# Attention groups 8 to 47 with P divided before the split, and P times V in four column tiles

## The reference

```
query = q @ w_q.T;  key = k @ w_k.T;  value = v @ w_v.T      # q is layernorm(x), k = v = ctx
scores = einsum("bghnd,bgsd->bghns", query, key) / 32 ** 0.5
scores = where(mask, scores, finfo.min)
attention = softmax(scores, axis=-1)
out = einsum("bghns,bgsd->bghnd", attention, value)
x = x + out.reshape(b, n, 1024) @ w_out.T
x12 = layernorm(x) @ w12.T + b12;  x1, x2 = split(x12, 2)
x = x + (silu(x1) * x2) @ w3.T + b3
```

## Time and profile before

| | |
|---|---|
| three runs | 1041.37, 1043.22, 1044.38 us; median 1043.22 |
| profiled execution, span from first to last instruction | 1040.4 us |
| PE busy | 1017.7 us, 98% of the span |
| DVE, POOL, ACT busy | 661.6, 498.6, 447.3 us (64%, 48%, 43%) |
| chain of work that ended last | PE 87%, DVE 6%, DMA 1%, ACT 1% |
| granted TensorE clock | 9 or more tenths in every slice, mean 0.998 |

### The profile page before, as it was taken

How to read it: one execution, slowest core, us unless ns; L and a number is a source line. 1 busy time by engine, 2 the same in 40 slices (tenths; PEclk the granted TensorE clock), 3 DMA queues, 4 the chain that set the end, 5 groups by cost and what they waited for, 6 DMA issues and landing times.

```text
span 1040.4 us, 21876 instructions
## 1 busy us (share of the span) xinstructions
PE 1017.7 (98%) x8400; PEld 695.6 (67%) x8400; DVE 661.6 (64%) x2080; ACT 447.3 (43%) x983; POOL 498.6 (48%) x476
## 2 busy tenths in 40 slices
PE   7897999999999999999999999999999999999998
PEld 6786868869687696886655544444444888468853
DVE  6789977767787777888646234636864447625431
ACT  6768556557465574664766210123431112202100
POOL 2869923727337273379958596158742301212000
PEclk9999999999999999999999999999999999999999
DMA  9669686998989999789946715494758631974201
GB/s 367 227 160 197 168 216 168 222 247 222 248 211 229 230 245 244 179 236 232 268 94 123 253 71 203 94 345 160 272 200 185 235 112 40 236 230 122 83 31 51
DMA packets 230776, 199.12 MB, mean 191 GB/s; under 512 B 177040, under 2 KB 187280, under 8 KB 225808
## 3 DMA queue, kind: packets, MB, share of 16 engines
q1 hardware_dynamic: 230672, 197.72, 69.0%
HBM read 119.04 MB, written 35.65 MB: 149 GB/s over the span
## 4 chain that ended last, share of the span: by engine, by line
PE 87%; DVE 6%; DMA 1%; ACT 1%; issue 0%; SPq 0%; DVEq 0%
PE bank_dense L1349 52%; PE bank_spare L1349 13%; PE bank_score L1494 6%; PE bank_spare L1494 6%; PE bank_av L1494 3%; PE bank_score L1406 2%; DVE arena_attn L1820 2%; DVE arena_attn L1830 1%; PE bank_av L1424 1%; PE bank_av L1428 1%; PE bank_av L1426 1%; PE bank_dense L1366 1%; DMA k_scratch<-arena_in 1%; PE bank_spare L1358 0%; PE bank_dense L1358 0%
## 5 line engine op out<-in xcount | busy, mean ns | idle before, releaser
L1153 ACT ACTIVATE arena_attn<-arena_attn,arena_in 128x128 f32<-128x128 f32 x512 | 162.7, 391 | 94.6 <-DVE arena_in L1820 93.6
L1349 PE MATMUL bank_dense<-arena_rows,arena_in 128*128 128x256 f16 (+1 forms) x1272 | 175.2, 295 | 1.9 <-POOL arena_in L874 1.0
L936 POOL TENSOR_TENSOR arena_attn<-arena_attn 128x512 f16<-128x512 f32 x89 | 102.6, 1170 | 148.8 <-ACT arena_attn L1160 148.8
L1349 PE MATMUL bank_dense<-arena_attn,arena_rows 128*128 128x512 f16 x768 | 166.4, 379 | 0.0
L1349 PEld LDWEIGHTS bank_dense<-arena_rows,arena_in 128*128 128x128 f16 x1272 | 123.0, 98 | 43.1 <-DVE arena_in L1668 1.6
L1820 DVE CUSTOM_DVE_ANT_0 arena_attn<-bank_score,arena_in 128x128 f32<-128x128 f32 x512 | 143.5, 346 | 0.4 <-PE bank_score L1406 0.4
L1349 PEld LDWEIGHTS bank_dense<-arena_attn,arena_rows 128*128 128x128 f16 x768 | 75.2, 98 | 90.2
L1349 PE MATMUL bank_dense<-arena_out,arena_attn 128*128 128x512 f16 x576 | 127.8, 379 | 0.0
L1349 PEld LDWEIGHTS bank_dense<-arena_out,arena_attn 128*128 128x128 f16 x576 | 55.5, 98 | 63.3
L1349 PE MATMUL bank_spare<-arena_rows,arena_in 128*128 128x256 f16 (+1 forms) x648 | 87.6, 292 | 0.0
L1349 PE MATMUL bank_dense<-arena_out,arena_in 128*128 128x512 f16 x384 | 83.0, 379 | 0.0
(11 more groups left out here) (219 smaller groups left out, 1890.8 us busy)
## 6 DMA issues: line engine op xcount, KB each, us to landing
arena_rows<-x SPq DMA_DIRECT2D x32, 512.0 KB, 6.1
arena_in<-w_scratch SPq DMA_DIRECT2D x64, 256.0 KB, 3.1
arena_attn<-q_scratch SPq DMA_DIRECT2D x48, 256.0 KB, 4.5
arena_rows<-w_t SPq DMA_DIRECT2D x12, 1024.0 KB, 6.2
arena_rows<-ctx_t SPq DMA_DIRECT2D x8, 1024.0 KB, 6.1
q_scratch<-arena_attn SPq DMA_DIRECT2D x16, 512.0 KB, 5.1
x_scratch<-arena_rows SPq DMA_DIRECT2D x16, 512.0 KB, 3.8
arena_out<-x_scratch SPq DMA_DIRECT2D x16, 512.0 KB, 5.9
```

The source lines that it names most:

```text
L936: ins = pool.tensor_tensor(p_split[:, g % 2, u, 1], e[:, g % 2, u], p_split[:, g % 2, u, 0], ALU.subtract)
L1153: ins = act.activation(head, head, ACT.Exp, bias=neg_max[:, g % 2, h:h + 1], scale=-1.0)
L1349: ins = pe.matmul(dst, lhs(a, c), rhs(b, c), start=(c == chunks[0] and n == 0), stop=(c == chunks[-1] and n == 2))
```

## The change

For groups 8 to 47 (`NORMED`, blocks 2 to 6) P is divided by its row sums before it is split. The row sum comes from the accumulator of the exponentials on ACT. In steps 0 and 1 of a block DVE divides (`by_vector`), in steps 2 to 7 POOL (`by_pool`; the reciprocal is a power of -1); P is scaled by 2 to the 14th. `prob_hi` then waits for the division instead of the exponentials. P times V has V as the stationary operand (128 by 32) and P streams (128 columns); the four heads of a group go to four column tiles of the array, and so to four quarters of the partitions, which is the layout that `out_proj` needs. So `weigh(g)` writes a dense bank, takes the place of `turn_attn(g)` in the middle of step `g + 3`, and `divide` and `turn_attn` are gone for these groups. SP's wait for `weigh(g - 2)` in `turn_prob` becomes a wait for this later place.

```diff
+NORMED = range(8, 48)
+P_SCALE = 2.0 ** 14
+def by_vector(g):
+    return g in NORMED and g % GROUPS < 2
+def by_pool(g):
+    return g in NORMED and g % GROUPS >= 2
...
+        def weighed(g):
+            return (s_dense, done("a", g)) if g in NORMED else (s_av, divided_count(g))
...
 def turn_prob(g):
                 if g >= 2:
-                    sp.wait_ge(s_av, g - 1)
+                    sp.wait_ge(*weighed(g - 2))
...
             # POOL
+            def norm_prob(g):
+                n = normed_count(g - 1, by_pool)
+                for u in range(U):
+                    pool.wait_ge(s_exp, 2 * g + u + 1)
+                    pool.tensor_scalar(inv_pool[:, u], p_sum[:, g % 2, u], 1 / P_SCALE, None, ALU.mult).then_inc(s_pinv, 1)
+                    pool.wait_ge(s_pinv, 2 * (U * n + u) + 1)
+                    pool.tensor_tensor(inv_pool[:, u], inv_pool[:, u], minus_one.broadcast_to([P, HPG]), ALU.pow)\
+                        .then_inc(s_pinv, 1)
+                    pool.wait_ge(s_pinv, 2 * (U * n + u) + 2)
+                    heads = e[:, g % 2, u].rearrange("p (j n) -> p j n", j=HPG)
+                    ins = pool.tensor_tensor(heads, heads, inv_pool[:, u].rearrange("p (j o) -> p j o", o=1)
+                                             .broadcast_to([P, HPG, SEQ]), ALU.mult)
+                ins.then_inc(s_pnorm, 1)
                     if GROUPS * (t - 1) + s > PLO_ALONE:
                         prob_lo(GROUPS * (t - 1) + s - 1)
+                    if by_pool(GROUPS * (t - 1) + s):
+                        norm_prob(GROUPS * (t - 1) + s)
...
             # ACT
                     head = e[:, g % 2, u, SEQ * j:SEQ * j + SEQ]
+                    if g in NORMED:
+                        ins = act.activation(head, head, ACT.Exp, bias=neg_max[:, g % 2, h:h + 1], scale=-1.0,
+                                             accum_out=p_sum[:, g % 2, u, j:j + 1])
...
             def prob_hi(g):
-                act.wait_ge(s_exp, 2 * g + 2)
+                if by_pool(g):
+                    act.wait_ge(s_pnorm, normed_count(g, by_pool))
+                elif by_vector(g):
+                    act.wait_ge(s_vnorm, normed_count(g, by_vector))
+                else:
+                    act.wait_ge(s_exp, 2 * g + 2)
...
             # PE, weigh(g)
+                if g in NORMED:
+                    dst = begin("a", g)
+                    terms_of_out = ((v_high, 0), (v_low, 0), (v_high, 1))
+                    for u in range(U):
+                        for n, (v, piece) in enumerate(terms_of_out):
+                            for j in range(HPG):
+                                ins = pe.matmul(dst[DH * j:DH * j + DH, SEQ * u:SEQ * u + SEQ],
+                                                v[:, a % 2, u, m, 0:DH], prob_t[:, g % 2, u, piece, j],
+                                                start=n == 0, stop=n == 2, tile_position=(0, DH * j))
+                    ins.then_inc(s_dense, 1)
+                    return
...
-                    if g >= 3:
+                    if g >= 3 and g - 3 in NORMED:
+                        weigh(g - 3)
+                    elif g >= 3:
                         turn_attn(g - 3)
...
-                    if g >= 2:
+                    if g >= 2 and g - 2 not in NORMED:
                         weigh(g - 2)
...
             # DVE
+            def norm_prob(g):
+                n = normed_count(g - 1, by_vector)
+                for u in range(U):
+                    dve.wait_ge(s_exp, 2 * g + u + 1)
+                    dve.reciprocal(inv_vector[:, u], p_sum[:, g % 2, u]).then_inc(s_vinv, 1)
+                    dve.wait_ge(s_vinv, U * n + u + 1)
+                    heads = e[:, g % 2, u].rearrange("p (j n) -> p j n", j=HPG)
+                    ins = dve.scalar_tensor_tensor(out=heads, in0=heads, scalar=P_SCALE,
+                                                   in1=inv_vector[:, u].rearrange("p (j o) -> p j o", o=1)
+                                                   .broadcast_to([P, HPG, SEQ]), op0=ALU.mult, op1=ALU.mult)
+                ins.then_inc(s_vnorm, 1)
             def divide(g):
+                if g in NORMED:
+                    return
...
                         attn_lo(g - 3)
+                    if by_vector(g):
+                        norm_prob(g)
```

More of the change, by code:

```diff
@@ L302, in later_unit, with normed_count, divided_count @@
     return UNITS * (f - PLAIN) + i
+def by_vector(g):
+    return g in NORMED and g % GROUPS < 2
+def by_pool(g):
+    return g in NORMED and g % GROUPS >= 2
+def normed_count(g, kind=lambda n: n in NORMED):
+    return sum(kind(n) for n in range(g + 1))
+def divided_count(g):
+    return g + 1 - normed_count(g)
 def plo_count(g):
@@ L1362, in turn_attn @@
             def turn_attn(g):
-                pe.wait_ge(s_avread, g + 1)
+                pe.wait_ge(s_avread, divided_count(g))
                 dst = begin("a", g)
```

35 lines of the change are left out of this document (25 added, 10 removed).

## The result

The changed kernel takes 1075.4 us (median of four runs, 1072.0 to 1077.2) against 1043.7 us: the ratio is 1.030, 95% interval 1.026 to 1.033. It is slower by 31.7 us, where 13 were forecast. The profiled execution has a span of 1074.6 us, 34.2 more than that of before.

What follows compares the result with a forecast made beforehand. PE was taken to bound blocks 2 to 6, busy in all of block 3's 64.65 us. The terms -2 + 6 + 1 + 8 = +13 us on 1043.2 gave 1056 us, slower by 1.2%, range 1030 to 1088.

Steps and rivals of the forecast that it cites:

- rival C: Blocks 2 to 6: POOL becomes the bound, its power paying for each column; +47 us, about 1090; chance 0.11.
- A: The forecast itself, the sum of the terms: 1056 us, slower by 1.2%; chance 0.40.
- D: New `weigh` on PE: tiles go one after another, 1.52 us each, +27 us and the stalls, 1085 us; chance 0.13.
- PE's list, -2 us: PE, 40 groups: new `weigh` 0.80 us replaces 0.84 of `weigh` and `turn_attn`; -2 us, between -20 and +27.
- Rival B: New `weigh` on PE: tiles stream side by side, 0.33 us or 0.53 with shape change; faster, 1037 us; chance 0.25.
- Block 2, +6 us: Block 2, steps 0 and 1: DVE's `norm_prob` ahead of the old divisions, 3.0 us a step; +6 us (3.8 to 7.5).
- The +1 us for later blocks: Steps 0 and 1 of the four later blocks: PE waits for DVE only at step 3's output projection; +1 us.
- Step 7, +8 us: Step 7 of five blocks: PE waits 1.6 us for `v_lo`, as ACT is late behind POOL; +8 us (6 to 12).
- `prob_hi` 2.0 us late: End of step 6 on ACT: `prob_hi` starts at 235.2 instead of 233.23, after POOL's division of 2.3 us.
- Hidden work: POOL's list grows from 30.7 to some 58 of 64.65 us a block; no wait of PE while POOL keeps up.
- The load whose lateness I thought covered by DVE's idle time: SP's load behind `turn_prob`: some 2 us late, DVE standing still that long, covered by its 16 us idle a block.
- The sign that I named for C: What would show rival C: POOL's power over 1.5 us and POOL busy over 90% of a block.

Runs made afterwards that it cites:

- clock kept: The changed kernel with PE turning the identity 24 and 12 times in step 7 of blocks 3 to 6: 1071.4 us, ratio 1.028.
- the best version found: Against the change: reciprocals early on DVE, loads and the b12 reduction reordered, only groups 11 to 39 without each block's step 6 changed: 1038.2 us, 0.996.

## Why the prediction was wrong in size

The direction was right, but 13 us were forecast and 31.7 measured, and the mechanism that set the time was rival C's, POOL as the bound, not A's. The time lay in the range because the range had been drawn up to C and D, so this speaks neither for the sum nor for A. By steps, blocks 2 to 6 took 33 us more: the five steps 7 32.3, steps 0 to 3 of block 2 4.0, waits in steps 4 and 5 of blocks 3 to 6 5.3, and the other 31 steps 8.3 less.

1. **PE's list, -2 us.** Wrong value between the right bounds: -10.8 by the run with the tiles alone. I had taken 0.80 us for `weigh` from the pace of the old load and matmul pairs; it takes 0.84 - 0.26 = 0.58, its 24 matmuls being six rounds of four, one round each 57 ns: 14 ns a matmul, below the old pairs' 25. The 0.2 us that I added for the change of the array's shape were near: 0.58 less six rounds of 57 ns leaves 0.24. Rival B's mechanism was right and decided nothing, since PE no longer bound the blocks. The Trainium skill's page "TensorEngine Tiling (Array Packing)", section Instruction Overhead, puts some 60 cycles on each matmul, 25 ns at 2.4 GHz by an estimate from that page. The trace does not agree for tiles side by side: 57 ns for a round of four are 14 ns a matmul, and the measurement decides. The estimate from the Trainium skill's page "TensorE: Matmul & The Clock Gate", Part 3, was 67 ns a round and 0.40 us; the rows above show 57 ns a round, 0.34 us for six.

2. **Block 2, +6 us.** Right in mechanism and near in size (rows below, answer to the earlier trace rows): steps 0 to 3 cost 4.0 us more (6.67 to 7.24, 6.66 to 8.42, 7.34 to 8.64, 9.11 to 9.45). DVE's products took 0.78 and 1.32 us in the first step, 2.4 us with the reciprocals, and not the 3.0 that I took. The +1 us for later blocks was not there.

```profile
120.80 0.78 DVE L1915 SCALAR_TENSOR_TENSOR arena_attn<-arena_attn 128x512 f32<-128x512 f32 x1
...
121.71 1.32 DVE L1915 SCALAR_TENSOR_TENSOR arena_attn<-arena_attn 128x512 f32<-128x512 f32 x1
...
125.01 0.44 PE L1428 MATMUL bank_dense<-arena_in 128*128 128x128 f32 x2 [1.68 <-DVE arena_in L1927]
```

3. **Step 7, +8 us.** This is the step that failed: the five steps 7 took 32 us more. The wait for `v_lo` was as forecast (1.61 us), but ahead of it stood 3.1 us for `scale_rows`, which I had followed in ACT's list and not to PE, and behind it the low clock. The error under both is "`prob_hi` 2.0 us late". It was 5.9 us late, because I let POOL divide the first sequence as soon as its exponentials were there. In POOL's list the division stands behind `prob_lo` of the group before, which waits for that group's `prob_hi`, which waits for its division. The lateness is there at the end of step 2 (7.8 us) and is handed on from step to step; that step 2 alone makes it is not shown, since the run with step 2's division on DVE did not decide.

4. **Hidden work.** "No wait of PE as long as POOL keeps up" was the right condition, and I answered it with POOL's busy time, 58 of 64.65 us (measured: 59.9). What counts is the chain. POOL's groups in block 3 of the change, by line:

```profile
L972 POOL TENSOR_TENSOR arena_attn<-arena_attn 128x512 f16<-128x512 f32 x16 | 18.2, 1157 | 6.1 <-ACT arena_attn L1222 6.1
L985 POOL TENSOR_TENSOR arena_attn<-arena_attn 128x512 f32<-128x512 f32 x12 | 12.5, 1039 | 0.9
L981 POOL TENSOR_TENSOR arena_attn<-arena_attn 128x4 f32<-128x4 f32 x12 | 12.4, 1036 | 1.0
```

POOL waits 6.1 us for `prob_hi` (and 1.4 for `exps`), which in turn wait for POOL; with these answers and the gaps between its operations its list fills the block. The load whose lateness I thought covered by DVE's idle time was not covered either: DVE stood 3.1 us for it in step 4 of its list, and PE up to 1.1 us for `mask_scores` of step 5 behind it.

```profile
226.82 2.29 DVE L1731 TENSOR_REDUCE arena_in<-arena_rows 128x1 f32<-128x2048 f32 x1 [3.10 <-DMA arena_rows<-w_t]
```

5. **Rival C.** Its condition did not come true (the power took 1.04 us, not the 1.63 of a price for each column), and yet POOL became the bound: the formula was nearly right and its threshold was worked out wrongly. 30.7 + 6 x (2n + 1.1) reaches 64.65 us at n = 2.28 us a sequence, that is at a power of about 0.94 us by the same terms (0.19 + 1.05 + 0.1 beside it), not 1.3. My own 1.0 us was past it. The whole division of a sequence took 2.5, and the formula with this gives 30.7 + 6 x 6.1 = 67.3; with the splits drawn out and the gaps it was 70.4 (clock kept) to 71.5. The sign that I named for C, POOL busy in over 90%, was wrong too: 84% was enough.

## What to carry to other kernels

Before work is moved to an engine with much idle time, follow its list once around: if what it is given waits, over another engine, for what it has itself just done, the period of that loop counts, not the busy share, and 84% busy can be full. When a loop is opened by another order, look for the next one, over the buffers (here the two of `e`). And a saving on the engine that bounds the kernel is only paid out as long as it stays the bound: here the tiles were worth 10.8 us alone, nothing beside the division, and 4.7 us in the best version found.

## What the runs showed of the hardware

- Matmuls to different column tiles do not start in the order of the list: with three in a row for each tile they still started four at a time, 57 ns from round to round, in the same time. The Trainium skill's page "TensorE: Matmul & The Clock Gate", Part 3, The mechanism, has matmuls start strictly in program order, with only weight loads pulled ahead. The rows of that run do not agree, and the measurement decides.
- A power on 4 columns on POOL takes 1.04 us, on one column 0.55; a product of 128 x 512 takes as long as the 4-column power.
- Behind a wait of PE of 3.1 us the granted clock was 0.64 and 0.59 over 8.8 us, between the levels of 2.4 GHz and 1.2 GHz, so work right behind a stall ran slower than its rows elsewhere (four turns of x 1.12 us). With the wait filled by turns of the identity it stayed at 1.00 in that step, and the same four turns took 0.60.
